# Sharing the edge products of a graph layer between GpSimd and VectorE

## What is computed

```python
h = (x @ W).reshape(G, Jn, H, C)
es = jnp.einsum('gjhc,hc->gjh', h, a_s)[:, src]
ed = jnp.einsum('gjhc,hc->gjh', h, a_d)[:, dst]
e = jax.nn.leaky_relu(es + ed, 0.2)
...
alpha = w / den[:, dst]
out = jnp.zeros((G, Jn, H, C), e.dtype).at[:, dst].add(alpha[..., None] * h[:, src])
```

## Time and profile before

| | |
|---|---|
| median of three runs | 6320.32 us |
| the profiled execution | 6291.15 us |
| its span, first to last instruction | 6289.4 us |
| VectorE busy | 5690.2 us (90%) |
| GpSimd busy | 4763.9 us (76%) |
| TensorE busy | 3906.9 us (62%) |
| ScalarE busy | 3244.1 us (52%) |
| products of the edges, L276 | 888, 471.3 us |
| additions of the edges, L565 | 592 narrow, 224.4 us; 296 wide, 214.0 us |

### The profile page before, as it was taken

The page is one execution under the profiler, slowest core; times in us unless marked ns, Lnnn a source line. Parts: engine busy times, 40 slices in busy tenths (PEclk is TensorE's granted clock), DMA queues, the critical chain, the costliest instruction groups (busy, mean ns, idle before and its releaser), DMA issues. The chain is left out here.

```text
span 6289.4 us, 59390 instructions
## 1 busy us (share of the span) xinstructions
PE 3906.9 (62%) x13720; PEld 2243.3 (36%) x13720; DVE 5690.2 (90%) x7312; ACT 3244.1 (52%) x5534; POOL 4763.9 (76%) x3337
## 2 busy tenths in 40 slices
PE   3412333156767767677676776766767766576777
PEld 3212322133333334333343333433333333255556
DVE  5788678859999999999999999999999999887778
ACT  1312132245666666666666656656666665544445
POOL 5263333359999999999999999999999999733334
PEclk8756576579999999999999999999999999988778
DMA  1000000034444444444444444444444444300000
GB/s 27 1 11 1 2 1 11 11 124 159 164 166 159 173 159 165 165 161 171 160 166 163 160 165 166 166 165 158 165 166 161 168 160 171 115 3 2 2 2 2
DMA packets 171481, 694.93 MB, mean 110 GB/s; under 512 B 27969, under 2 KB 34626, under 8 KB 171138
## 3 DMA queue, kind: packets, MB, share of 16 engines
q1 hardware_dynamic: 169608, 688.25, 30.0%
q0 software_dynamic: 1536, 3.14, 0.2%
HBM read 684.77 MB, written 6.55 MB: 110 GB/s over the span
## 5 line engine op out<-in xcount | busy, mean ns | idle before, releaser
L1032 PE MATMUL m_PS<-m_pr,ident 128*128 128x512 f32 (+1 forms) x6144 | 2497.5, 544 | 906.4 <-DVE m_pr L1156 906.1
L816 POOL TENSOR_TENSOR m_hs<-m_u,m_BC 128x1280 f32<-128x1280 f32 x1024 | 2991.2, 2921 | 62.1 <-DVE m_u L1173 62.1
L1148 DVE TENSOR_TENSOR_SCAN m_hs<-m_PS,m_hs 128x640 f32<-128x640 f32 x2048 | 2937.6, 1469 | 5.8 <-POOL m_hs L816 3.8
L873 ACT ACTIVATE m_PS<-m_dt,m_A 128x640 f32<-128x640 f32 x2048 | 1613.4, 794 | 912.2 <-DVE m_hs L1148 898.6
L1032 PEld LDWEIGHTS m_PS<-m_pr,ident 128*128 128x128 f32 x6144 | 1135.0, 195 | 2168.6 <-DVE m_pr L1156 1133.2
L823 POOL TENSOR_TENSOR m_pr<-m_hs,m_BC 128x384 f32<-128x384 f32 x1024 | 1085.5, 1060 | 184.3 <-DVE m_hs L1148 179.1
L1156 DVE TENSOR_TENSOR m_pr<-m_hs,m_PS 128x896 f32<-128x896 f32 x1024 | 1082.5, 1057 | 8.4 <-DVE m_hs L1148 7.0
L276 POOL TENSOR_TENSOR g_prod<-g_hbuf,g_E 128x128 f32<-128x128 f32 (+1 forms) x888 | 471.3, 568 | 633.8 <-ACT g_E L328 606.7
L862 ACT COPY m_PS<-m_BC 128x448 f32<-128x448 f32 x1024 | 546.4, 534 | 155.9 <-DVE m_pr L1156 107.6
L1357 POOL TENSOR_SCALAR f_negm<-f_top 128x1 f32<-128x1 f32 x160 | 33.5, 209 | 444.7 <-DVE f_top L1557 260.5
L362 PE MATMUL g_TB<-ident,g_nrm 128*128 128x128 f32 x200 | 64.1, 322 | 443.8 <-DVE g_nrm L498 439.1
(11 more groups left out here) (241 smaller groups left out, 4330.0 us busy)
## 6 DMA issues: line engine op xcount, KB each, us to landing
m_BC<-m_scr SPq DMA_DIRECT2D x1024, 640.0 KB, 3.7
m_scr<-m_CB SPq DMA_DIRECT2D x32, 160.0 KB, 4.2
m_hs<-in_cwr SPq DMA_DIRECT2D x4, 512.0 KB, 3.9
out<-f_res SPq DMA_DIRECT2D x20, 64.0 KB, 1.5
m_inw<-in_in_w SPq DMA_DIRECT2D x4, 256.0 KB, 3.8
m_dtw<-in_dw SPq DMA_DIRECT2D x4, 256.0 KB, 3.5
m_xw<-in_xw SPq DMA_DIRECT2D x8, 64.0 KB, 3.6
m_outw<-in_ow SPq DMA_DIRECT2D x4, 128.0 KB, 3.3
```

What stands on the lines that cost most here:

```text
L816: pool.tensor_tensor(hs[:, g % RH], u[:, p % 2], BC[:, g % UB:g % UB + 1, 0:S].to_broadcast([P, DT, S]), ALU.mult).then_inc(w_ready, 1)
L873: act.activation(half[d], dt_[:, p % 2, d], ACT.Exp, scale=A[:, l, d, n:n + 1]).then_inc(da_ready, 1)
L1032: ins = pe.matmul(Y[:, a:e], ident[:], pr[:, g % RP, a:e], start=False, stop=False, skip_group_check=True)
L1148: v.tensor_tensor_scan(hs[:, g % RH, d, :], half[d], hs[:, g % RH, d, :], 0.0, ALU.mult, ALU.add).then_inc(scan_done, 1)
```

## The change

VectorE makes a part of the products itself: of the narrow layers' edges every fourth (`e % 4 == 3`), of the wide layer's every third (`e % 3 == 2`). GpSimd leaves these out. VectorE issues the product of edge `e + 1`, if it is its own, ahead of the addition of edge `e`. Its products count a semaphore of their own, `own_ready`. As VectorE now needs the source nodes too, the second row of packed numbers holds both ends of two edges, in four fields of 6 bits; GpSimd's row stays as it was. VectorE reloads its registers at edge 95 in place of 96, and waits for the exponentials ahead of the loop.

```diff
+        SHARE = [4, 3, 4]
+        def own(l, e):
+            return e % SHARE[l] == SHARE[l] - 1
...
+        def field(eng, reg, regs, e, first, bits, size):
             packed = regs[e // 2 % KEEP]
+            if first:
+                eng.reg_alu(reg, packed, first, ALU.logical_shift_right)
+                packed = reg
+            if first + bits < size:
+                eng.reg_alu(reg, packed, (1 << bits) - 1, ALU.bitwise_and)
...
+        def source_of_four(eng, reg, regs, e):
+            return field(eng, reg, regs, e, BITS + e % 2 * BITS, BITS, 24)
+        def target_of_four(eng, reg, regs, e):
+            return field(eng, reg, regs, e, e % 2 * 3 * BITS, BITS, 24)
...
                         for e in range(NE):
                             if e == 2 * KEEP:
                                 load(pool, src, 0, KEEP, NPK)
-                            j = node(pool, here, src, e)
+                            if own(l, e):
+                                continue
+                            j = source(pool, here, src, e)
...
-                chain(v.scalar_tensor_tensor(pack[:], nodes[:, :, 1:NE:2], float(SHIFT), nodes[:, :, 0:NE:2], ALU.mult, ALU.add))
+                chain(v.scalar_tensor_tensor(pack[:, 0, :], nodes[:, 0, 1:NE:2], float(SHIFT), nodes[:, 0, 0:NE:2], ALU.mult, ALU.add))
+                chain(v.scalar_tensor_tensor(low[:, 0, :], nodes[:, 0, 0:NE:2], float(1 << BITS), nodes[:, 1, 0:NE:2], ALU.mult, ALU.add))
+                chain(v.scalar_tensor_tensor(low[:, 1, :], nodes[:, 1, 1:NE:2], float(1 << BITS), nodes[:, 0, 1:NE:2], ALU.mult, ALU.add))
+                chain(v.scalar_tensor_tensor(pack[:, 1, :], low[:, 1, :], float(SHIFT), low[:, 0, :], ALU.mult, ALU.add))
...
+                        v.wait_ge(sm_act, lp * N_SA + N_SA)
+                        def product(e):
+                            j = source_of_four(v, here, dst, e)
+                            ins = v.tensor_tensor(
+                                slots[:, e % SLOTS[l]].rearrange("p b (h c) -> p b h c", c=C),
+                                hb[l][:, :, bass.ds(j, 1), :].rearrange("p b o (h c) -> p b (o h) c", c=C),
+                                E[:, :, :, e:e + 1].to_broadcast([P, 2, H, C]), ALU.mult)
+                            ins._wait_ge(added, lp * NE + max(e + 1 - SLOTS[l], 0) + RING)
+                            ins.then_inc(own_ready, 1)
                         for e in range(NE):
-                            if e == 2 * KEEP:
+                            if e == 2 * KEEP - 1:
                                 load(v, dst, 1, KEEP, NPK)
-                            j = node(v, there, dst, e)
-                            v.wait_ge(prod_ready, lp * NE + e + 1)
+                            j = target_of_four(v, there, dst, e)
+                            if e + 1 < NE and own(l, e + 1):
+                                product(e + 1)
+                            if own(l, e):
+                                v.wait_ge(own_ready, made_before(lp, True) + made(l, e + 1, True))
+                            else:
+                                v.wait_ge(prod_ready, made_before(lp, False) + made(l, e + 1, False))
                             to = av[:, :, bass.ds(j, 1), :].rearrange("p b o c -> p b (o c)")
                             ins = v.tensor_tensor(to, to, slots[:, e % SLOTS[l]], ALU.add)
                             ins._wait_ge(added, lp * NE + e + RING)
```

More of the change, by code:

```diff
@@ L38, in embed_stage @@
     RING = 4
-    SHIFT = 4096
+    SHIFT, BITS = 4096, 6
     NPK = NE // 2
@@ L45, in embed_stage @@
     LOW = -3.0e38
-    assert J % 2 == 0 and NE % 2 == 0 and NPK < 2 * KEEP and P < NE <= KEY and 2 * J <= P
+    assert J % 2 == 0 and NE % 2 == 0 and NPK < 2 * KEEP and P < NE <= KEY and J <= 1 << BITS and 2 * J <= P
     with ExitStack() as ctx:
@@ L96, in embed_stage @@
         pack = at(M, 7 * P, 2, NPK)[0:1]
+        low = at(F, 0, 2, NPK)[0:1]
         pack_i = sb("pack_i", [1, 2, NPK], I32)
@@ L159, in embed_stage, with made, made_before @@
         sm_pe, sm_act, sm_dve = sem("sm_pe"), sem("sm_act"), sem("sm_dve")
-        prod_ready, added = sem("prod_ready"), sem("added")
+        prod_ready, own_ready, added = sem("prod_ready"), sem("own_ready"), sem("added")
+        SHARE = [4, 3, 4]
+        def own(l, e):
+            return e % SHARE[l] == SHARE[l] - 1
+        def made(l, e, by_vector):
+            return sum(own(l, i) == by_vector for i in range(e))
+        def made_before(lp, by_vector):
+            return sum(made(i % 3, NE, by_vector) for i in range(lp))
         rows_done = sem("rows_done")
@@ L183, in ring_of, with source @@
             return prod[:].rearrange("p q b c -> p (q b c)").rearrange("p (q b c) -> p q b c", b=2, c=COUT[l])
-        def node(eng, reg, regs, e):
+        def field(eng, reg, regs, e, first, bits, size):
             packed = regs[e // 2 % KEEP]
[L188 to L192, removed]
-                                      skip_runtime_bounds_check_because="the numbers are clamped to J - 1 before they are packed")
+            if first:
[3 more added lines that the diff above has]
+                eng.reg_alu(reg, packed, (1 << bits) - 1, ALU.bitwise_and)
+            return nc.s_assert_within(eng.snap(reg, min_val=0, max_val=(1 << bits) - 1), 0, J - 1,
+                                      skip_runtime_bounds_check_because="the numbers are clamped to J - 1 before they are packed")
+        def source(eng, reg, regs, e):
+            return field(eng, reg, regs, e, e % 2 * 12, 12, 24)
+        def source_of_four(eng, reg, regs, e):
+            return field(eng, reg, regs, e, BITS + e % 2 * BITS, BITS, 24)
+        def target_of_four(eng, reg, regs, e):
+            return field(eng, reg, regs, e, e % 2 * 3 * BITS, BITS, 24)
         def in_turn(*steps):
@@ L475, in _ @@
                 dst = [v.alloc_register(f"g_dst{q}") for q in range(KEEP)]
-                there = v.alloc_register("g_there")
+                here, there = v.alloc_register("g_here_v"), v.alloc_register("g_there")
                 keepf_f = keepf[:].rearrange("p h e -> p (h e)")
@@ L558, in _ @@
                         slots = ring_of(l)
+                        C = n // H
+                        v.wait_ge(sm_act, lp * N_SA + N_SA)
[7 more added lines that the diff above has]
+                            ins.then_inc(own_ready, 1)
                         for e in range(NE):
-                            if e == 2 * KEEP:
+                            if e == 2 * KEEP - 1:
                                 load(v, dst, 1, KEEP, NPK)
-                            j = node(v, there, dst, e)
-                            v.wait_ge(prod_ready, lp * NE + e + 1)
+                            j = target_of_four(v, there, dst, e)
[5 more added lines that the diff above has]
+                                v.wait_ge(prod_ready, made_before(lp, False) + made(l, e + 1, False))
                             to = av[:, :, bass.ds(j, 1), :].rearrange("p b o c -> p b (o c)")
```

## The result

The changed kernel takes 6382.37 us (median, 6374.51 to 6386.61) against 6321.24 us before: 1.0095 of it, 95% interval 1.0077 to 1.0112. It is 61 us slower; the prediction said 50 us, 6370.5 us, in a range of 6310 to 6402 us.

A forecast was written before the change was run, and what follows sets the result against it. It took the edge loops to be bounded by turns of VectorE and GpSimd. Narrow 34.5, wide 15.0 and setup 0.7 us sum to +50.2 us; on 6320.3 that is 6370.5 us, range 6310 to 6402 us.

The forecast's parts named there:

- The loops are bounded by turns: Six edge loops: VectorE and GpSimd alternate, one product and one addition in each turn, 0.417 us narrow and 0.767 wide.
- A group costs three turns and two additions alone: Four narrow edges: 3 x 0.417 + 2 x 0.325 = 1.901 us, +0.233; three wide: 2 x 0.767 + 2 x 0.46 = 2.454, +0.153.
- The product takes what an addition takes: VectorE's added product in the loops: the addition's 0.29 us narrow, 0.43 wide; least step around it 0.21 and 0.35.
- The rest is free: Waits and the moved reload cost nothing; setup's packing instructions add +0.7 us.
- The queue adds: Rival, loops: uncovered register work costs each of 246 products 0.115 us more than the sum, +28 us, 6399 us; chance 0.12.
- Shorter turns: Rival, loops: the shared thing alone sets the pace, VectorE's latency always filled; -22 and -23 us, 6276 us; chance 0.13.
- behind the stage nothing changes: After the changed stage, ending near 1250 us: nothing changed, so a microsecond won or lost there is one of the whole.

The follow-up runs named there:

- mute: Kernel before, but GpSimd writes a constant into each slot instead of making the product, reading nothing (output wrong): 6154.88 us, six loops 371.6 us.
- relay: Kernel before, but ScalarE copies each product from its SBUF slot to one of eight PSUM banks, where VectorE adds it: 6202.29 us, 0.9849 of before.
- wide_all: The change, but VectorE makes every product of the wide layer and GpSimd none there; narrow layers all on GpSimd: 6306.3 us, 0.9965 of before.
- ahead2: The change, but VectorE issues its product ahead of the addition two edges before it, not one; reload at edge 94: 6373.15 us, 1.0076 of before.
- dense: The change with every second product on VectorE in all layers: 6344.12 us, 47.5 over before, one execution.
- fixed: The change, but VectorE's products all read node 7, without register work for the source (output wrong): 6341.68 us, 45.0 over before, one execution.
- none: The change with no product on VectorE, its packing, wait and earlier reload kept: 6325.68 against 6323.88 us, 1.0002 of before.
- b_again: The kernel before, unchanged, run once more for a second profile: 6320.65 us.
- relay_four: Kernel before with products copied by ScalarE to PSUM and four node numbers packed into one, so no reloads: 6186.08 us, 0.9826 of before.

## Why the prediction was right, point by point

The sign, the place and the mechanism (turns) were right, and the range held the time. Where the turns fall within a group was wrong, and that the sum came out to the hundredth in spite of it is luck.

- *The loops are bounded by turns.* Right, and the runs add that the turns are over reading SBUF, shown from three sides: without GpSimd's reads VectorE steps at 0.326 us (`mute`), with additions that read PSUM GpSimd goes at 0.587 us (`relay`), and without GpSimd VectorE needs 0.67 us an edge for both (`wide_all`).
- *A group costs three turns and two additions alone.* 1.901 us predicted, 1.900 measured; wide 2.454 predicted, loops +7.6 us against +7.5. But the pieces are others. The sum had three narrow steps of 0.417 and two of 0.325 us; measured are one of 0.417, one of 0.325, one of 0.403, one of 0.527 and one of 0.228. The turn ahead of the product is covered by the register work (0.403 us from addition to product; the row-by-row estimate was 0.44). The one behind the product costs 0.20 us, not 0.09, since product and addition follow each other without latency to hide it. And the addition behind the product starts after 0.228 us, since it does not wait for the product, where the sum had a dependent step of 0.325. In the wide group two steps of 0.767 and two of 0.46 turn out as 0.878, 0.712, 0.460 and 0.404. In both sizes the errors cancel. So the sum was right, but "a turn's price and two dependent steps" is a way to count this order, not a law: `ahead2` has the same pieces and another wide sum, and `dense` pays less for each product.
- *The product takes what an addition takes.* Right where no turn falls on it: 0.30 us in the narrow loops of the change, 0.42 us in `wide_all`. In the wide loops of the change a turn does fall on it, and it lasts 0.77 us. The least step between independent instructions, 0.21 and 0.35 us, was measured as 0.209 (`fixed`) and 0.336.
- *The rest is free.* `none`: 1.0002.
- *The queue adds* was priced too high: 0.44 - 0.325 = 0.115 us holds for the 148 narrow products, but the wide step in the sum was 0.46 us, which covers the 0.44. By its own terms this rival is 17 us over the sum and not 28, and the top of the range about 6388 us in place of 6402. The measured 6382.37 us lies under both. `fixed` shows that the register work is not what the change lost.
- *Shorter turns* (6276 us) failed: VectorE's latency is not always filled. The narrow group has a dependent step of 0.325 us that carries no turn, the wide one such a step of 0.460 us. The rule of the Trainium skill (SBUF — State Buffer, SBUF: two separate sides) that the shared pair of ports is held for a whole instruction is not what these rows show, as far as its length goes: 0.417 us a pair, where the two lengths make 0.70. By the Trainium skill (SBUF — State Buffer, Who interferes with whom) a VectorE instruction with two SBUF inputs contends with a GpSimd instruction that reads SBUF and not with one that only writes it. This agrees with `mute` (additions of 291 to 294 ns next to GpSimd's writes) and with `relay` (286 to 290 ns with one SBUF input, next to GpSimd's products).
- *What was missing: 11 us.* The loops account for 49.9 of the 61 us. Between two profiled executions with the long setup, `b_again` and the change, the difference is 66.0 us: 49.9 in the loops, 1.7 in the setup, 0.1 in the rest of the stage, and 14.3 behind it, where the program is the same. About 7 us of those arise in the first 88 us of the Mamba stage. At the same distance from its start, 40 to 62 us, first the change and then `b_again`:

```profile
1368.40:1390.40 22.00, 17.54 (x67) 13.69 (x66) 0.00 (x0) 3.64 (x9) 0.00 (x0) 0.65 0.00 1
```

```profile
1316.80:1338.80 22.00, 14.51 (x67) 11.16 (x66) 0.00 (x1) 6.58 (x12) 0.00 (x0) 0.81 0.00 1
```

The 67 matmuls take 17.5 us at a mean granted clock of 0.65 and 14.5 us at 0.81: TensorE is granted 2.4 GHz later, counted from the start of the stage. `ahead2` and `wide_all` have it as well (mean clock 0.64 and 0.63 there), `none` does not (0.81). The length of the loops, in which TensorE is idle, does not decide it. `fixed` has loops as long as the change's and the clock of the kernel before:

```profile
1335.50:1357.50 22.00, 14.76 (x68) 10.97 (x66) 0.00 (x0) 6.37 (x12) 0.00 (x0) 0.81 0.00 0
```

`relay_four` has much shorter loops and the late grant (0.64 in the same stretch, 40 to 62 us behind the start). In `fixed` and `dense` the whole kernel lost what the loops lost, within 2 us. So the term that was mis-sized is "behind the stage nothing changes", put at 0, but no run shows that its 11 us belong to the products. Why the grant comes later in some kernels, and where the other half of the 14 us arises, stays open.

## What to carry to other kernels

Two engines that are both busy and in step with each other, each slower than alone, may be taking turns at something, as here. Then giving a part of the work from one to the other saves nothing as long as both keep reading there: every share tried, from every eighth product to every second, lost time. Look for the operand that can be read elsewhere (here PSUM, through an idle ScalarE), or let one engine do all of it. Share out work when one engine alone sets the pace: then the same kind of move that lost 7.6 us a wide loop won 3.

## What the runs showed of the hardware

- Two operations with two SBUF inputs each, one on VectorE and one on GpSimd, take turns for a part of their length: 128 elements cost 0.417 us for the pair, 256 cost 0.767, against 0.325 and 0.46 us for VectorE alone and 0.37 and 0.587 for GpSimd alone. GpSimd's writes (`mute`) and VectorE additions with one input in PSUM (`relay`: 286 to 290 ns in 376 of them) are not touched.
- The GpSimd turn that finds two VectorE instructions back to back costs 0.20 us, in a latency gap 0.09 us (0.527 and 0.417 against 0.325 us). With 256 elements it is 0.42 and 0.31 us (0.878 and 0.767 against 0.46 us).
- VectorE's setup ran at up to 1.4 us from one instruction to the next in the profiles of the change and of the four kernels after it, and at about 0.25 us in that of before and in the eight later ones, whatever the kernel. It is worth 27 us; a single profiled execution can lie that far from the median.
- The granted clock of TensorE over the same 22 us of the Mamba stage was 0.81 in some kernels and 0.63 to 0.65 in others, though the program is the same there, and it did not follow the length of the loops ahead (0.81 in `fixed`, 0.64 in `relay_four`). With it the change fell about 7 us behind `b_again`.
- ScalarE's copies to PSUM take 0.27 and 0.38 us, and eight banks, one slot each, let VectorE catch up with its 5.8 us reload in part: taking the reload away on top still gave 3.7 us a narrow loop (59.3 to 55.6).
